# Forming the rounding rest of ln(1+e) as one tile on ScalarE and GpSimd, so that TensorE sums three tiles for dt

## What is computed

```
x = x + replace_by_nearest_word(groupnorm(x))   # 256 words of 256 channels, nearest by cosine, kept if close
x = x + mamba_layer(groupnorm(x))
# mamba_layer: layer norm over channels, the channels in 4 chunks of 64; for each chunk
#   xi, z = in_proj(chunk);  xc = silu(causal_conv4(xi) + conv_b)           (128 inner channels)
#   dt = softplus(dt_proj(x_proj_dt(xc)) + dt_b);  B, C = x_proj_BC(xc)     (16 states)
#   h[t] = exp(dt[t]*A) * h[t-1] + dt[t]*xc[t]*B[t];  y[t] = sum_s h[t]*C[t]
#   out = out_proj((y + xc*D) * silu(z)) + skip*chunk
# then layer norm and a 256x256 projection
```

## Time and profile before

| | us |
|---|---|
| median of 3 runs | 4431.4 (4430.06 to 4437.95) |
| the profiled execution's own time | 4433.55 |
| its span, first to last instruction | 4431.7 |
| VectorE busy | 4003.7 |
| TensorE busy | 3779.5 |
| GpSimd busy | 3427.9 |
| ScalarE busy | 2810.5 |

### The profile page before, as it was taken

One profiled execution on the slowest core, in us unless ns is written; L12 is line 12 of the kernel. 1 busy time (PEld: TensorE's weight loads), 2 busy tenths in 40 slices (PEclk: granted clock), 3 DMA queues, 4 the chain that ended last, 5 costly groups with the idle time before them and its releaser, 6 DMA issues. The chain is left out here.

```text
span 4431.7 us, 44302 instructions
## 1 busy us (share of the span) xinstructions
PE 3779.5 (85%) x13840; PEld 1269.6 (29%) x13840; DVE 4003.7 (90%) x3073; ACT 2810.5 (63%) x3528; POOL 3427.9 (77%) x2086
## 2 busy tenths in 40 slices
PE   3688988988888898888989888888988988888896
PEld 2222323223232232323223232232323323232221
DVE  2589899998989999899999989999899998989996
ACT  2566666666666666666666666666666666666653
POOL 2487787787878878888778788787788778788775
PEclk8898998999989999998999989999998999989997
DMA  1657576675757758576675767757576675767763
GB/s 39 154 143 193 149 189 177 174 192 152 190 157 188 201 135 202 148 192 180 167 197 143 200 159 186 201 140 202 140 196 183 164 197 144 198 162 186 193 166 109
DMA packets 217723, 751.74 MB, mean 170 GB/s; under 512 B 27400, under 2 KB 28816, under 8 KB 213392
## 3 DMA queue, kind: packets, MB, share of 16 engines
q1 hardware_dynamic: 217488, 748.91, 65.7%
HBM read 639.75 MB, written 75.50 MB: 161 GB/s over the span
## 5 line engine op out<-in xcount | busy, mean ns | idle before, releaser
L592 POOL TENSOR_TENSOR state<-state,c_all 128x1024 f32<-128x1024 f32 x1024 | 2400.1, 2362 | 252.0 <-DVE state L953 229.5
L953 DVE TENSOR_TENSOR_SCAN state<-dtb,ub 128x1024 f32<-128x1024 f32 x1024 | 2341.0, 2286 | 42.7 <-ACT dtb L795 6.1
L1182 PE MATMUL ub<-u,spr 64*128 64x512 f32 x4096 | 1271.5, 683 | 352.1 <-DVE state L953 349.6
L795 ACT ACTIVATE dtb<-dtb,a_neg 128x1024 f32<-128x1024 f32 x1024 | 1159.7, 1141 | 389.4 <-DMA dtb<-dt_scratch 379.8
L944 DVE TENSOR_TENSOR ub<-ub,b_all 128x1024 f32<-128x1024 f32 x1024 | 1243.1, 1214 | 105.0 <-PE ub L1182 98.8
L1182 PEld LDWEIGHTS ub<-u,spr 64*128 64x128 f32 x4096 | 347.8, 196 | 1160.2 <-DVE state L953 679.6
L1198 PE MATMUL yp<-state,gat 128*32 128x512 f32 x4096 | 583.0, 643 | 6.1 <-POOL state L592 6.1
L1047 PE MATMUL mb<-xs,wtap 128*128 128x512 f32 x512 | 261.4, 657 | 20.1 <-DMA xs<-xn 10.6
L668 ACT ACTIVATE dt<-mb 128x512 f32<-128x512 f32 x128 | 75.8, 592 | 241.7 <-PE mb L1078 241.7
L643 ACT ACTIVATE e_x<-mb,ncb 128x512 f32<-128x512 f32 x128 | 88.0, 687 | 219.1 <-PE mb L1047 219.1
L1061 PE MATMUL mb<-xc,wdt 128*128 128x512 f32 x256 | 153.1, 683 | 78.3 <-ACT ym L715 55.4
(11 more groups left out here) (143 smaller groups left out, 4821.6 us busy)
## 6 DMA issues: line engine op xcount, KB each, us to landing
dtb<-dt_scratch SPq DMA_DIRECT2D x1024, 512.0 KB, 4.8
xs<-xn SPq DMA_DIRECT2D x128, 256.0 KB, 5.3
b_all<-bc_scratch SPq DMA_DIRECT2D x64, 512.0 KB, 6.4
c_all<-bc_scratch SPq DMA_DIRECT2D x64, 512.0 KB, 7.9
xt<-in_x SPq DMA_DIRECT2D x16, 1024.0 KB, 6.6
x_scratch<-xt SPq DMA_DIRECT2D x16, 1024.0 KB, 7.0
dt_scratch<-dt SPq DMA_DIRECT2D x64, 256.0 KB, 3.4
dt_scratch<-dt SPq DMA_DIRECT2D x128, 128.0 KB, 3.6
```

The source lines that it names most:

```text
L592: pool.tensor_tensor(v, v, c_all[:, c % 2, :], ALU.mult).then_inc(gated, 1)
L795: act.activation(dtb[:, k, :], dtb[:, k, :], ACT.Exp, scale=a_neg[:, GROUP[g]:GROUP[g] + 1]).then_inc(decayed, 1)
L953: dve.tensor_tensor_scan(state[:, g % STATES, :], dtb[:, k, :], ub[:, g % 2, :], 0.0, ALU.mult, ALU.add).then_inc(scanned, 1)
L1182: last = pe.matmul(ub[:, g % 2, h * HALF:(h + 1) * HALF], spr[lo:lo + TURN, GROUP[g] % 8, :], u[lo:lo + TURN, c % 2, h * HALF:(h + 1) * HA ...
```

## The change

ScalarE does one more pass: `prep_dt_less` at step 18, ahead of the logarithm, takes 1 from `e_z` in place. GpSimd's `prep_dd` stays at step 16 of its list, waits for that pass and forms e - ((1+e)-1) in `e_z` with a tensor-tensor subtraction, where it took 1 from `e_z` with a tensor-scalar instruction. TensorE's `prep_dt` waits for that tile and adds it alone, one product in place of two. The negative identity `nidf`, its input and its load go, so the weights are 17 loads in place of 18.

```
-           17: ["prep_dt_exp", "prep_dt_one"], 18: ["prep_dt_ln", "prep_bc0"], 19: ["prep_bc1"], 21: ["prep_dt0"],
+           17: ["prep_dt_exp", "prep_dt_one"], 18: ["prep_dt_less", "prep_dt_ln", "prep_bc0"], 19: ["prep_bc1"], 21: ["prep_dt0"],
...
                 elif name == "prep_dd":
-                    pool.wait_ge(dt_one, m + 1)
-                    hold_here(pool)
-                    pool.tensor_scalar(e_z[:], e_z[:], 1.0, -1.0, ALU.mult, ALU.add).then_inc(dt_less, 1)
+                    pool.wait_ge(dt_less, m + 1)
+                    pool.tensor_tensor(e_z[:], e_x[:], e_z[:], ALU.subtract).then_inc(dt_rest, 1)
...
+                elif name == "prep_dt_less":
+                    act.wait_ge(dt_one, m + 1)
+                    act.activation(e_z[:], e_z[:], ACT.Identity, bias=minus[:, 0:1]).then_inc(dt_less, 1)
...
                 elif name.startswith("prep_dt"):
-                    pe.wait_ge(dt_less, m + 1)
+                    pe.wait_ge(dt_rest, m + 1)
                     bank = banks(kind, b, (name, c))[0]
-                    pe.matmul(mb[:, bank, :], idf[:], e_x[:, cut], start=False, stop=False)
-                    pe.matmul(mb[:, bank, :], nidf[:], e_z[:, cut], start=False, stop=True).then_inc(m_full[bank], 1)
+                    pe.matmul(mb[:, bank, :], idf[:], e_z[:, cut], start=False, stop=True).then_inc(m_full[bank], 1)
```

More of the change, by code:

```diff
@@ L179, in build @@
 def build(nc, x, words, cols, w_in, w_z, w_taps, w_bc, w_dt, w_xdt, w_out, w_proj,
-          iota, ident_f, ident_b, ident_neg, diag_d, group_mean, spread, gather, out):
+          iota, ident_f, ident_b, diag_d, group_mean, spread, gather, out):
     x_v = x.rearrange("b (j p) h w -> b p j (h w)", p=P)
@@ L256, in build @@
         idf = sb("idf", [P, P])
-        nidf = sb("nidf", [P, P])
         dd = sb("dd", [P, 2, P])
@@ L316, in build @@
         dt_less = sem("dt_exp_rounded")
+        dt_rest = sem("dt_exp_rest")
         dt_ln = sem("dt_ln")
@@ L372, in _ @@
                      (wo[:], w_out), (wp[:], w_proj), (idf[:], ident_f),
-                     (idb[:], ident_b), (nidf[:], ident_neg), (dd[:], diag_d), (grp[:], group_mean), (spr[:], spread),
+                     (idb[:], ident_b), (dd[:], diag_d), (grp[:], group_mean), (spr[:], spread),
                      (gat[:], gather), (iot[:], iota)]
@@ L810, in _ @@
             act.preload_act_table_set("natural_log_exp_and_others")
-            act.wait_ge(s_w, 16 * 18)
+            act.wait_ge(s_w, 16 * 17)
             act.activation(a_neg[:], col[:, C_ALOG:C_ALOG + NS], ACT.Exp)
@@ L825, in _ @@
             for name in ("prep_xc0", "prep_xc1", "prep_sig_x", "prep_raw0", "prep_raw1", "prep_dt_exp", "prep_dt_one",
-                         "prep_dt_ln", "prep_bc0", "prep_bc1", "prep_dt0", "prep_dt1"):
+                         "prep_dt_less", "prep_dt_ln", "prep_bc0", "prep_bc1", "prep_dt0", "prep_dt1"):
                 do(name, "pro", -1, NC - 1)
@@ L971, in _ @@
             dve.memset(mean_w[:], 1.0 / CH)
-            dve.wait_ge(s_w, 16 * 18)
+            dve.wait_ge(s_w, 16 * 17)
             for k in range(2):
@@ L1222, in turn @@
                             do(name, kind, b, c)
-            pe.wait_ge(s_w, 16 * 18)
+            pe.wait_ge(s_w, 16 * 17)
             pe.wait_ge(su_pe_ready, 1)
@@ L1297 @@
         "ident_f": np.eye(P, dtype=np.float32), "ident_b": np.eye(P, dtype=ml_dtypes.bfloat16),
-        "ident_neg": -np.eye(P, dtype=np.float32), "diag_d": diag_d,
+        "diag_d": diag_d,
         "group_mean": np.kron(np.eye(P // 8, dtype=np.float32), np.full((8, 8), 0.125, np.float32)),
```

## The result

The changed kernel takes 4485.2 us (median of 4 runs, 4482.65 to 4495.83) against 4432.3 for the kernel before in the same comparison: ratio 1.0122, interval 1.0103 to 1.0141. It is slower by 53 us; the forecast was 58.6 us slower (4490), with a range of 4464 to 4528. The profiled execution's own time is 4486.22, its span 4484.4, its mean granted clock 0.930 (before 0.932).

A forecast was written before the change was run, and what follows sets the result against it. VectorE was taken as the bound, with GpSimd lacking slack in the second chunk. 63.6 (second chunk) -4 (first chunk) -1 (rest) = +58.6 us, giving 4490 for the median; range 4464 to 4528.

The forecast's parts named there:

- Steps 1 and 2: Second chunk: ScalarE's moment pass and dt copy slip 3.7 us behind the x2 addition; VectorE's second u product stalls 3.0.
- Step 3: Second chunk: GpSimd's clamp, moments, Newton step and everything from squares to variance come 4.54 us later; VectorE takes it in full.
- step 2: Second chunk: VectorE's second u product waits for ScalarE's late copy of dt's second half, a stall of 3.0 us.
- rival (a): TensorE's clock falls in the second chunk after the u product stall; 5.7 to 6.9 us a batch, 4515 us; chance 0.15.
- about 2 us in most: Second chunk: VectorE's wait at the variance in the kernel before, about 2 us in most batches.
- the rule on the clock gate: TensorE's clock is halved when it idles and returns with sustained work; fewer passes and a stall could cost more than they free.
- the bound of 1.24: ScalarE's new pass, taken as 1.06 us; at 1.24 the second chunk would cost 4.7 us a batch.
- -0.3: First chunk: net gain of 0.3 us a batch, -4 us in all, bounds -0.9 and +0.95.
- the -1 of the sum: Batch 0 and the last batch cost about 1 us together, which start-up gives back; the sum takes -1.
- the +29: Worst low case: 3.0 us a batch in the second chunk with the first chunk's -0.9, 42-13.
- (b): Second chunk: misread slack hides the 4.54 us lag, leaving first-chunk effects within 0.2%; 4430 us, chance 0.06.
- (c): Faster: lag hidden, and VectorE waited for TensorE's passes at units 13 to 15, first chunk; 20 us, 4411, chance 0.05.

The follow-up runs named there:

- the filler run: The changed kernel with four more identity products on TensorE just ahead of own_z in the second chunk of batches 1 to 14: 4503.5 us, ratio 1.0157.
- the one with the short pass: The changed kernel with GpSimd's subtraction replaced by a 1.04 us tensor-scalar instruction that sets the tile to zero: 4488.0 us, ratio 1.0117.

## Why the prediction was right

**The place and the mechanism were right.** The loss is in the second chunk of batches 1 to 14 and follows GpSimd's lag. GpSimd's idle time there is 6.71 us, as said (6.7), the lag 4.50 and 4.39 where 4.54 was worked out. Taking the lag away by moving c_scale takes the loss away; adding the wait alone brings most of it.

**Steps 1 and 2.** In 14 batches ScalarE's L704 waits for the x2 addition (2.6 to 3.4 us, 3.18 in batch 7) and the second u product for ScalarE (2.59 us); forecast 3.7 and 3.0. The forecast took the wait from today's start of L701 and counted no delay of ScalarE's own; in batch 7 ScalarE comes there 0.3 us later by itself, as the two decays behind dt's first copy take 2.42 us in place of 2.17.

**Step 3 was wrong in what comes last.** It said that the squares wait for the Newton steps 4.54 us later. In 13 batches they wait for c_proj instead, because TensorE stands idle in the lag, here mostly in the stall of step 2, and comes back at the lower level: rival (a) came true as far as the instructions go (c_proj 8.9 us a batch in place of 7.5), but not in its price, which it put at 5.7 to 6.9 us a batch. In batch 7 the squares came 6.26 us later for it. That the mean is 4.25 and not more has a second reason: before, TensorE's means for the variance ran at the lower level in 10 of the 14 batches, which made the waits of "about 2 us in most" that the prediction read, and after the change in one. VectorE's variance in these chunks waits 22.4 us in all before and 7.1 after, most of the 22.8 us that its wait lost. So the lower level costs 1.1 us a batch before (75.0 against 73.9) and, by the filler run's 77.9, 1.3 after, and nearly cancels in the difference; at full clock throughout the price is 4.0, where the 4.54 was to be taken in full. Here the rule on the clock gate that the prediction drew on from the Trainium skill ("TensorE: Matmul & The Clock Gate", "Part 1: The HAM clock gate") agrees with the trace in its direction: idle 3.04 us, then 5.42 us for what takes 3.70. In batch 4 the same wait (3.06 us) was followed by the full level, c_proj 7.4 us.

**The extra pass** took 1133 ns, not 1.06 us, which the bound of 1.24 had covered. The subtraction took 2359 ns as its row said.

**The first chunk.** The wait at unit 11 appeared (11.2 us in 14 waits, 0.8 each; forecast 0.7 to 0.95), and that at unit 13 (6.6 us) went. In sum the interval became 0.2 us longer, where -0.3 was taken: 7 us in all on the sum.

**The rest of the sum.** 59.5 us for the second chunk where 63.6 was forecast, +3 for the first where -4 was, and start-up and batch 0 at -6.3 where about -1 was. The terms are each off by 4 to 7 us and partly cancel, so that the total is within 6 us of the forecast is in part luck. Of the -6.3 us, 4.6 are two intervals of batch 0 (59.6 and 75.8 us before, 57.3 and 73.5 after), and the same two vary by as much from batch to batch within the kernel before. Two figures do not come out of their own working: the -1 of the sum, since the working has the start-up give that 1 us back, and the range's lower end, which by the +29 is 4460 and not 4464. Neither bears on the outcome.

**Rivals (b) and (c)** fell: waits at L704 and L868 are there, and the interval that holds the first chunk did not become shorter.

## What to carry to other kernels

An engine with 23% of idle time can have none for the next 28 us: look for the stretch in which its queue runs without a gap, and ask what a step in front of that stretch waits for. A change that moves a wait to another place in the releasing engine's list can cost more than the instructions that it adds (45 of 53 us here), and work that stands behind a wait without needing it can be put in front of it. Where a clock or a wait takes two values from batch to batch, compare the batches at the same value before a mean is explained. If a stall is moved away from one consumer and the time doesn't change, the lag has other ways to the same end.

## What the runs showed of the hardware

The mean granted clock of TensorE differs between executions of one kernel, and the time goes with it: of the ten executions of the changed kernel with c_scale at step 15 and the pass behind the logarithm, the one at 0.926 took 4449.7 us and the one at 0.937 took 4424.1. The profiled executions of all kernels lie between 0.923 and 0.938. So the size that one profile shows for a place outside the second chunk (75.0 to 76.2 us for the first between the changed kernel and the one with the short pass) can be that of the execution, and differences of 10 to 20 us between two kernels' medians stayed open above. An activation with a tile column as its bias took 1133 ns (L688, 64 instructions) against 1057 (L684) for the same shape with a constant.
